# A three-layer graph convolution in split single precision: the last 148 nodes as an eleventh pair of blocks, and W2's combined operands kept in SBUF

## What is computed

```python
h = jnp.maximum(_layernorm(x), 0.0)              # x: 2708 x 512
h = jax.nn.relu(adj @ (h @ W1) + b1)             # adj: 2708 x 2708, W1: 512 x 1024
h = jax.nn.relu(adj @ (h @ W2) + b2)             # W2: 1024 x 1024
return x + adj @ (h @ W3) + b3                   # W3: 1024 x 512
```

## Time and profile before

| what | value |
|---|---|
| median of 3 runs (lowest to highest) | 1592.18 us (1591.36 to 1593.42) |
| the profiled execution's own time | 1593.0 us |
| its span in the profile | 1591.2 us |
| PE busy | 1581.1 us, 99% |
| DVE, ACT, POOL busy | 872.1, 610.6, 456.3 us |
| mean DMA rate | 191 GB/s |

### The profile page before, as it was taken

One profiled execution on the slowest core, in us unless ns is written; L12 is line 12 of the kernel. 1 busy time (PEld: TensorE's weight loads), 2 busy tenths in 40 slices (PEclk: granted clock), 3 DMA queues, 4 the chain that ended last, 5 costly groups with the idle time before them and its releaser, 6 DMA issues.

```text
span 1591.2 us, 20930 instructions
## 1 busy us (share of the span) xinstructions
PE 1581.1 (99%) x7674; PEld 1360.1 (85%) x7674; DVE 872.1 (55%) x1361; ACT 610.6 (38%) x1076; POOL 456.3 (29%) x417
## 2 busy tenths in 40 slices
PE   9999999999999999999999999999999999999999
PEld 7788889988889898989898989788898888888898
DVE  8973433256553443434564446564565538766856
ACT  5442222234433332323332333443455536454444
POOL 5863544336654000000000015345402214201302
PEclk9999999999999999999999999999999999999999
DMA  6975657644567554545455658884645336887866
GB/s 244 321 225 205 222 179 220 204 138 152 176 220 235 151 153 143 142 118 148 143 169 161 175 186 282 275 298 133 206 120 133 93 93 202 251 249 220 252 191 198
DMA packets 196628, 303.37 MB, mean 191 GB/s; under 512 B 22632, under 2 KB 92608, under 8 KB 196524
## 3 DMA queue, kind: packets, MB, share of 16 engines
q1 hardware_dynamic: 162268, 223.12, 47.1%
q0 software_dynamic: 12224, 43.16, 8.4%
q10 hardware_dynamic: 22032, 35.74, 6.3%
HBM read 219.44 MB, written 82.50 MB: 190 GB/s over the span
## 4 chain that ended last, share of the span: by engine, by line
PE 91%; DVE 5%; DMA 3%; ACT 1%; issue 0%; ACTq 0%; DVEq 0%
PE ps L1731 30%; PE ps L1733 30%; PE ps L1732 30%; DVE slots L1350 1%; PE ps L1824 1%; DVE still L1332 1%; DMA H<-parts 1%; DVE stats L1279 1%; DMA raw<-adjT 0%; DMA raw<-W 0%; DVE ring L1360 0%; DMA raw<-TS 0%; DMA P<-stage_b 0%; DMA raw<-T 0%; ACT slots L1099 0%
## 5 line engine op out<-in xcount | busy, mean ns | idle before, releaser
L1360 DVE TENSOR_TENSOR ring<-raw,ring 128x512 fp32r<-128x512 f32 (+1 forms) x562 | 404.7, 732 | 426.6 <-ACT ring L1131 424.1
L1131 ACT CAST ring<-raw 128x512 fp32r<-128x512 f32 (+1 forms) x562 | 321.3, 577 | 561.9 <-PE ps L1733 464.8
L1731 PE MATMUL ps<-slots,still 128*128 128x512 f32 (+1 forms) x504 | 183.6, 364 | 2.3 <-DVE slots L1350 1.4
L1733 PE MATMUL ps<-slots,still 128*128 128x512 f32 (+1 forms) x504 | 183.1, 363 | 0.0
L1732 PE MATMUL ps<-slots,still 128*128 128x512 f32 (+1 forms) x504 | 183.1, 363 | 0.0
L1733 PE MATMUL ps<-ring,even 128*128 128x512 f32 (+1 forms) x480 | 174.6, 364 | 0.0
L1732 PE MATMUL ps<-ring,even 128*128 128x512 f32 (+1 forms) x480 | 174.6, 364 | 0.0
L1731 PE MATMUL ps<-ring,even 128*128 128x512 f32 (+1 forms) x480 | 174.6, 364 | 0.0
L1587 POOL DMA_DIRECT2D prep<-P x40 | 26.4, 662 | 465.2 <-DMA P<-U 434.4
L1731 PE MATMUL ps<-ring,S 128*128 128x512 f32 (+1 forms) x420 | 153.0, 364 | 0.6 <-DVE ring L1360 0.6
L1733 PE MATMUL ps<-ring,S 128*128 128x512 f32 (+1 forms) x420 | 152.5, 363 | 0.0
(11 more groups left out here) (162 smaller groups left out, 2891.1 us busy)
## 6 DMA issues: line engine op xcount, KB each, us to landing
raw<-TS SPq DMA_DIRECT2D x160, 256.0 KB, 2.9
raw<-adjT SPq DMA_DIRECT2D x138, 256.0 KB, 3.1
raw<-adjT SPq DMA_DIRECT2D x41, 512.0 KB, 4.6
TS<-made SPq DMA_DIRECT2D x20, 1024.0 KB, 6.6
raw<-TS SPq DMA_DIRECT2D x80, 165.0 KB, 2.4
raw<-HS SPq DMA_DIRECT2D x50, 256.0 KB, 2.7
raw<-P SPq DMA_DIRECT2D x45, 256.0 KB, 4.0
raw<-adjT SPq DMA_DIRECT2D x68, 165.0 KB, 2.6
```

What stands on the lines that cost most here:

```text
L1131: act.copy(hi, src).then_inc(hi_done, 1)
L1360: dve.tensor_tensor(lo, src, hi.bitcast(F32), ALU.subtract).then_inc(lo_done, 1)
L1731: pe.matmul(out, st_hi, mv_hi, start=start, stop=False)
L1733: return pe.matmul(out, st_lo, mv_hi, start=False, stop=stop)
```

## The change

- Blocks 20 and 21 become an eleventh pair (74 + 74 nodes), done in all seven parts. Its operands lie in DRAM in 128 rows each: 74 rows and the first 54 again in one stack, and rows placed to match in a second, so that two matmuls per bank (`extra_pair`) take the place of the four. The adj stacks come from a new input `adjX`, their combinations are made by POOL (`prep_extra`, kept in `TX`); the stacks of h1 and of the third layer go through `HX` and `HX3`. Every group of pass 2 and pass 3 now has a tail tile, a `left` tile (cut to its high half only) and, once a part in pass 2 and once a group in pass 3, a stationary stack. The group for part `None` is gone.
- In pass 3 the three finishes of a chunk that are not part 1's all stand behind the drain of part 4, and the store of part 4 waits for the last of them, nine cuts behind that drain.
- In w2 the combined operands of chunk 0 too are made in `hold`; the loads for the next quarter are issued ahead of the sums of this one. `parts` is used in halves that change places from chunk to chunk (`sides`).
- At the start the root and centring of block 1 stand behind the second half's cut of block 0.

```diff
+BLOCKS = [b for t in ORDER[:EARLY] + (EXTRA,) + ORDER[EARLY:] for b in ((20, 21) if t == EXTRA else (t, t + PAIRS))]
...
+def sides(chunk):
+    return (0, 4) if chunk % 2 == 0 else (4, 0)
...
 # pass2()
-                    if half is not None and i == (8 if g.inner else 6):
-                        tail_step(g, c, half)
+                    if i == 6:
+                        tail_step(g, c)
...
+                k = p.tile("left", True, low=False)
+                k.chunk, k.part = c, part
+                g.left, g.extra = k, at["extra", part]
...
 # pass3()
-            for part in (0, 1, 2, 3, None, 4, 5, 6):
+            for part in range(7):
...
+                    if i == 0:
+                        tail_step(g, c)
+                    spread_in(late)
+                    p.emit_due()
+                    if i == 2:
+                        k = p.tile("extra3", False)
...
+                k = p.tile("left", True, low=False)
...
 # drain3()
-        for where, half, side, last in {1: [(4, 0, 0, 1)], None: [(6, 1, 1, 4), (2, 0, 1, 5)],
-                                        4: [(0, 1, 0, 6)]}.get(part, []):
+        for where, half, side, last in {1: [(4, 0, 0, 1)],
+                                        4: [(2, 0, 1, 5), (0, 1, 0, 6), (6, 1, 1, 4)]}.get(part, []):
...
-            p.later(4 if part == 1 else 2, store)
+            p.later({1: 4, 4: 9}.get(part, 2), store)
...
 # ACT, store of pass 3
-                    if g.part == 1:
-                        act.wait_ge(finished, plan.final_of[g.chunk, 1])
+                    if g.part in (1, 4):
+                        act.wait_ge(finished, plan.final_of[g.chunk, g.part])
...
 # DVE, drain of part 4 in pass 3
-                                dve.scalar_tensor_tensor(C, bank, b3, C, ALU.add, ALU.add).then_inc(drained, 1)
+                                dve.scalar_tensor_tensor(C, bank, b3, Y, ALU.add, ALU.add).then_inc(drained, 1)
...
 # the start, ACT
-                        root(1)
-                        centre(1)
                         return
...
+                    if j.a == 1:
+                        root(1)
+                        centre(1)
...
 # POOL
+            def held_load(c, second, q, turn):
+                w = WIDTH[c]
+                pool.wait_ge(prep_done, state["done"])
+                pair = (prep[:, 0:2, 0:w], aux[:, :, 0:w])[turn]
+                prep_load(turn, P2[q, :, :].rearrange("p (a n) -> p a n", a=2)[:, :, within(c)], pair)
+                prep_load(2 + turn, P2[KF + q, :, columns(0 if second else 1, c)], prep[:, 2 + turn, 0:w])
+                return pair[:, 0, :], pair[:, 1, :], prep[:, 2 + turn, 0:w], turn, state["in"][turn::2]
...
             def prep_held(c):
+                ahead = None
+                for n in range(2 * KF):
+                    second, q = divmod(n, KF)
+                    if c == 0 and n == KF:
+                        pool.wait_ge(group_done, at["pass2_end"])
+                        for u in range(CHUNKS):
+                            pool.wait_ge(u_stored[u], 16 * KF)
+                    alone = c == 0 and n < KF
+                    mine = ahead or held_load(c, second, q, 0 if alone else n % 2)
+                    ahead = None
+                    if n + 1 < 2 * KF and not alone:
+                        ahead = held_load(c, *divmod(n + 1, KF), (n + 1) % 2)
+                    held_sums(c, second, q, mine)
...
 # PE
-            def left_over(g, ms, hi, lo, tail, side, started):
+            def extra_pair(g, ms, first, second):
                 j = g.left
                 w = WIDTH[g.chunk]
-                pe.wait_ge(lo_done, j.cut + 1)
+                pe.wait_ge(hi_done, j.cut + 1)
                 pe.wait_ge(tail_lo, g.tail[0])
                 for m in range(ms):
+                    cols = slice(m * P, (m + 1) * P)
+                    out = ps[:, g.banks[m], 0:w]
+                    pe.matmul(out, first[:, cols], ring[:, j.slot % RING, 0, 0:w], start=False, stop=False)
+                    pe.matmul(out, second[:, cols], slot_tails[g.tail[0] % 2][:, 0:w], start=False, stop=True) \
+                        .then_inc(group_done, 1)
```

More of the change, by code:

```diff
@@ L104, in later, with tile @@
         self.pending.sort(key=lambda q: q[0])
-    def tile(self, kind, ring, loads=1):
+    def tile(self, kind, ring, loads=1, low=True):
         j = Tile(kind, self.cuts)
         self.cuts += 1
+        if low:
+            self.lows += 1
+            j.low = self.lows
         if loads:
@@ L123, in take_raw @@
         before = self.raw_user[j.raw % RAW]
-        j.raw_freed = before.cut + 1 if before else None
+        j.raw_freed = before
         self.raw_user[j.raw % RAW] = j
@@ L410, in drain2 @@
             p.owed |= set(bufs)
-        if bufs and part != 4:
+        if bufs:
             def store():
@@ L504, in go @@
                 b = g.block
[L505 to L517, removed]
+                if EARLY <= pair_of(b) < PAIRS:
                     buf = ("stash", 2 * (b % PAIRS - EARLY) + b // PAIRS)
@@ L574, in pass3 @@
                 g = p.group("pass3", c, part, [2 * pair, 2 * pair + 1])
-                here = list(ORDER) if part is not None else []
-                half = {1: 0, None: 1, 5: 0, 6: 1}.get(part)
-                for t in here:
+                for i, t in enumerate(ORDER):
                     j = p.tile("moving", True)
@@ L948, in _, with wait_h1, extra_rows @@
             seen = {"p1": 0, "h2": -1}
+            waited = []
+            def wait_h1():
+                seen["h1"] = 1
+                for i in range(PAIR_BUFS):
+                    sp.wait_ge(kept_stored[i], kept(i, PAIRS + 1))
+                    sp.wait_ge(sums_stored[i], sums(i))
+            def extra_rows(part, c, row):
+                if part in DIRECT:
+                    k, a = DIRECT[part]
+                    return adjX[k, row, :, columns(a, c)]
+                i = {S2: 3, S3: 1, S1: 0, X22: 2}[part]
+                if ("tx", c) not in seen:
+                    seen["tx", c] = 1
+                    for k in (0, 2):
+                        sp.wait_ge(prep_out[k], 32 * (c + 1))
+                return TX[row, i, :, within(c)]
             def load(j):
@@ L1117, in cut @@
                     act.wait_ge(group_done, 8 * CHUNKS)
+                if j.kind == "extra2" and j.part == X11:
+                    act.wait_ge(made_done, 4 * made_total)
+                    act.wait_ge(lo1_done, len(tiles1))
+                if j.kind == "extra3":
+                    act.wait_ge(g_stored[0], plan.stored["g", 0])
                 if j.kind == "w2s" and j.part == S2:
@@ L1832, in pass2_group @@
                         pe.wait_ge(stat_lo, plan.stat_of["h1", j.pair, g.part])
-                    pe.wait_ge(lo_done, j.cut + 1)
+                    pe.wait_ge(lo_done, j.low)
                     s = j.slot % RING
-                    end = g.left is None and n == PAIRS - 1
                     for m in range(KF):
```

546 lines of the change are left out of this document (269 added, 277 removed).

## The result

The changed kernel takes 1617.76 us (median of 4 runs, 1614.86 to 1620.27); the ratio to before is 1.0154, with a 95% interval of 1.0141 to 1.0166. Slower was forecast, at 1604 and at most 1611.

A forecast was written before the change was run, and what follows sets the result against it. The kernel was taken as bound by PE's count of matmuls. Terms -7.3 - 1.4 - 1.8 + 0 + 0.3 + 0 + 18.3 + 4 gave +12.1 us, 1604.3 for the median (predicted 1604), range 1595 to 1611.

The forecast's parts named there:

- The store of part 4 in pass 3: Pass 3: ACT stands in this store until POOL's third finish and PE runs dry, once a chunk; +18.3 us (15 to 22).
- The clock in those holes: Pass 3's three store holes: PE's clock falls to half, 1.35 us a hole; +4 us (0 to 8).
- Rival 1: Store holes in pass 3 open but PE's clock recovers at once, or POOL is quicker; +8 us or less; chance 0.23.
- rival 2: Pass 3: the ring hides POOL's three finishes, done before PE runs dry; -10 us, 1582; chance 0.16.
- Matmuls: Passes 2 and 3: two matmuls replace four per bank, twelve fewer per chunk, taken from PE itself; -7.3 us.
- h1 to pass 2: Step into pass 2: two stack cuts delay the third moving tile, other extra transfers hidden; +0.3 us (0 to +0.5).
- More transfers in pass 3: Pass 3: denser loads, some 275 GB/s, starve the narrow chunk about as much as the old holes; 0 (-1.4 to +4).
- rival 3: Pass 3 becomes bound by transfers, raw buffers turning slower than PE eats, worst in the narrow chunk; 1610; chance 0.11.
- w2, chunk 0: w2: loads and stores of T go, so the hole at 1030 closes; -1.4 us (0 to -1.4).
- w2, halves of `parts`: w2: with `sides`, buffers were stored a part earlier, so the hole at 1155 closes; -1.8 us (0 to -1.8).
- Rival 4: w2: its holes stay, as W loads and H stores are unchanged; +3 us on any case; no chance of its own.
- The start: Kernel start: the hole at 9.66 closes but DVE limits up to 75 us, so paid back; 0 (-1.05 to +0.3).

The follow-up runs named there:

- e3: Changed kernel with each stacked store's transfers of 74 and 54 rows made as four of 64, 10, 48 and 6: 1610.58 us, 1.0117 of the kernel before.
- e4: Changed kernel with the first two stack loads of pass 2 behind tiles 5 and 8 in place of 1 and 3: 1610.45 us, 1.0117 of before.
- e10: Changed kernel with the edits of e3 and e4 together, part 4's store still at nine cuts: 1610.58 us, 1.0107 of the kernel before.
- e1: Changed kernel with pass 3's part 4 store eighteen cuts behind its drain in place of nine: 1603.25 us, 1.0066 of the kernel before.
- e8: Changed kernel with the edits of e1, e3 and e4 and the old order at the start: 1590.36 us, 0.9985 of the kernel before.
- e7: Changed kernel with block 1's root, centring and inverse back ahead of the second half's cut: 1615.12 us, 1.0137 of the kernel before.
- e2: Changed kernel with pass 3's part 4 store twelve cuts behind its drain in place of nine: 1607.78 us, 1.0097 of the kernel before.
- e6: e1 with only the first of pass 3's 21 tail tiles loaded and used for all: 1597.57 us, 1.0022 of the kernel before.
- e5: Changed kernel with the edits of e1, e3 and e4 together, the new start kept: 1594.19 us, 1.0003 of the kernel before.

## Why the prediction was wrong in size and right in kind

- *The store of part 4 in pass 3* and *The clock in those holes*: right in place and mechanism, with +18.3 and +4 forecast and 21.9 measured in sum. Their shares were off: PE stood about 14.4 us (POOL's three finishes took 15.9 us in place of 17.5) and lost 7.5 us to slow matmuls, 1.9 to 2.9 a hole in place of 1.35. That the sum came out within 0.4 us is luck: one share was 3.9 us too high, the other 3.5 too low. Of the bounds (0 to 2.7), the upper was the better one. The Trainium skill, "TensorE: Matmul & The Clock Gate", section Why this matters for your kernels, has it that an idle gap brings the halved clock back; the windows agree, 0.50. Rival 1, a clock that doesn't matter, is out. So is rival 2: POOL issued the loads only behind the adds.
- *Matmuls*: 36 fewer; -7.3 us fits the sum of the table.
- ***h1 to pass 2*: the step that failed.** It counted ACT's two stack cuts and forecast +0.3 us. It was 10.7. "The extra transfers are hidden" was said of the rest of pass 2, and the stores of the stacks were not looked at, though they are in the diff. Their 74 rows run on two engines, SP and POOL stand behind them, and what both had to do then came in the same 20 us. e3, e4 and e10 show it: 10.7 us to 4.1, 8.1 and 2.5. The 0.3 us for ACT's two cuts wasn't measured by itself.
- *More transfers in pass 3*: 0 forecast with +4 as its bound. In the changed kernel the rest of pass 3 lost 2.7 us more than before. With the stalls away it is 8.1 us more (e1), 6.9 in e8. The likely reason is the one said against rival 3, that the buffers fill while ACT stands, so that the two costs don't add; no run isolates it. The rate forecast was right: some 275 GB/s, and e8 has 275 from 1312 to 1412 us. The term is mis-sized beyond its bound once the store is mended; for the kernel as it stands it was within it, and rival 3, as the main cause, is out.
- *w2, chunk 0* and *w2, halves of* `parts`: both holes of the earlier trace rows are gone, -3.2 us as forecast. But one new hole of 2.7 us stood in the changed kernel's profile. PE's timeline, and the chain ahead of it:

```profile
1055.32 0.39 PE L1814 MATMUL ps<-ring,W2c 128*128 128x512 f32 x1
1058.15 0.47 PE L1812 MATMUL ps<-ring,W2c 128*128 128x512 f32 x1 [2.44 <-DVE spill L1566]
```

```profile
1048.94 6.55 DMA H<-spill
```

  A drain waited for a store of `spill` that took 6.55 us. Of the ten other profiles none has it (at most 0.9 us of w2 holes), so it is a matter of the execution; what made the store slow that once stays open. Rival 4 is out.
- *The start*: 0 forecast with +0.3 as its bound. The hole at 9.66 closed, and one of 0.66 us opened near 13, so 0.4 us was gained. That it is paid back at 68 isn't shown: the hole there was smaller in the changed kernel's profile than before (0.5 and 1.3 us), and the medians of e7 and e8 alone speak for a cost of some 3 us.

In sum, forecast against measured: matmuls -7.3 and -7.3; w2 -3.2 and -0.5; store and clock 22.3 and 21.9; h1 to pass 2 0.3 and 10.7; pass 3 otherwise 0 and 2.7; start up to 246 us 0 and -1.9 in that one profile. The range ended at 1611 because no term in it allowed for a transfer that runs on a few engines. One reading of the trace before was short too: the other holes make some 3 us only from 20 us on, and some 4.4 us more, much the same in both kernels, are lost ahead of the hole at 9.66.

## What to carry to other kernels

A count of rows in a transfer is a matter of time: 74 rows left two of sixteen DMA engines at work, and what costs is less the transfer than the queues that stand behind it and the crowd that forms when they move on. Check the stores that a change adds as closely as its loads. And of two limits close together, a stall hides the other: repair it, and expect part of the gain to come back as the next wait.

## What was not expected of the hardware

- Behind a store of 74 rows the DMA share was 0.13 at 40 to 50 GB/s, and a store of L900 landed 14.6 us after its issue; in rows of 64, 10, 48 and 6 the longest took 7.5 us.
- PE's clock fell after a hole of only 2.0 us (e2 and e8), 0.8 to 1.3 us after the work had resumed, and stayed at 1.00 behind a hole of 3.4 us. This is PE's timeline in e7, where the granted clock is 1.00 from 68 to 76 us:

```profile
68.16 0.39 PE L1812 MATMUL ps<-slots,still 128*128 128x512 f32 x1
71.81 0.50 PE L1810 MATMUL ps<-slots,still 128*128 128x512 f32 x1 [3.27 <-DVE still L1407]
```

  Near 68 it fell behind holes of 2.6 to 2.9 us (e1, e3, e6, e10) and stayed behind 2.8, 3.1 and 3.4 (e5, e2, e7). It fell in every hole of 3.9 us and more, and in none under 1.9. What decides between isn't shown. At the earlier trace rows it fell 2.7 us after the last matmul.
- A fall cost 1.9 to 2.9 us of slow matmuls behind the changed kernel's holes of 4 to 7 us, and 1.6 to 2.9 over all kernels.
